# A perceiver block: the first query projection from high and low parts, the rotation's addition on GpSimd, scores laid out by chunk

## The reference

```
q_hk  = (layernorm(x) @ Wq.T)          # 16 heads of 128
q_big = einsum(q_hk, w_kc_q)           # per head: 128 -> 384
q_big = rope(q_big)                    # x*cos + rotate_half(x)*sin
q_r   = einsum(q_big, W_qr)            # per head: 384 -> 64
kv_r  = rope(ctx);  k_r = einsum(kv_r, W_kr)
p     = softmax(q_r @ k_r.T)           # 16 heads, 256 x 4096
out   = (p @ kv_r, then w_kc_kv, then Wo)
```

## Time and profile before

| | us |
|---|---|
| median of the runs | 1048.62 |
| the profiled execution, its time | 1046.65 |
| its span | 1044.70 |
| TensorE busy | 990.0 |
| VectorE busy | 734.7 |
| ScalarE busy | 575.3 |
| GpSimd busy | 290.8 |

### The profile page before, as it was taken

One profiled execution on the slowest core, in us unless ns is written; L12 is line 12 of the kernel. 1 busy time (PEld: TensorE's weight loads), 2 busy tenths in 40 slices (PEclk: granted clock), 3 DMA queues, 4 the chain that ended last, 5 costly groups with the idle time before them and its releaser, 6 DMA issues.

```text
span 1044.7 us, 17977 instructions
## 1 busy us (share of the span) xinstructions
PE 990.0 (95%) x6612; PEld 789.3 (76%) x6612; DVE 734.7 (70%) x1449; ACT 575.3 (55%) x1257; POOL 290.8 (28%) x210
## 2 busy tenths in 40 slices
PE   7999999999999799999999999999999999989996
PEld 5545689999997667588777878878888787868643
DVE  2566546555553679888887987978877787648555
ACT  3435344444442320287767767776676777836633
POOL 6910054444442300000002222422405423013422
PEclk9999999999999899999999999999999999999998
DMA  8560067665531332121013443424313203074100
GB/s 273 128 244 1 3 197 263 220 220 216 211 121 51 98 101 88 43 82 59 21 24 77 81 129 49 102 41 92 84 37 96 72 1 97 1 274 193 66 1 20
DMA packets 65981, 109.16 MB, mean 104 GB/s; under 512 B 19409, under 2 KB 44145, under 8 KB 64754
## 3 DMA queue, kind: packets, MB, share of 16 engines
q1 hardware_dynamic: 65906, 108.17, 34.0%
HBM read 103.24 MB, written 4.91 MB: 104 GB/s over the span
## 4 chain that ended last, share of the span: by engine, by line
PE 77%; DVE 13%; ACT 5%; issue 2%; DMA 1%; POOL 1%; SPq 0%; DVEq 0%; POOLq 0%; ACTq 0%
PE PS L1658 16%; PE PS L1531 12%; PE PS L1647 10%; PE PS L1635 8%; PE PS L1550 6%; PE PS L1620 4%; PE PS L1750 3%; DVE scores L1164 2%; PE PS L1672 2%; ACT scores L840 1%; PE PS L1431 1%; PE PS L1793 1%; PE PS L1590 1%; PE PS L1379 1%; PE PS L1599 1%
## 5 line engine op out<-in xcount | busy, mean ns | idle before, releaser
L1217 DVE TENSOR_TENSOR pL<-PS,pH 128x512 fp32r<-128x512 f32 x256 | 175.8, 687 | 63.3 <-ACT pH L864 62.9
L864 ACT ACTIVATE pH<-PS 128x512 fp32r<-128x512 f32 x256 | 151.8, 596 | 100.2 <-PE PS L1647 100.2
L840 ACT ACTIVATE scores<-scores,nmX 128x512 f32<-128x512 f32 x256 | 185.2, 724 | 18.5 <-DVE nmX L1168 18.5
L1164 DVE TENSOR_SCALAR_CACHE_REDUCE scores<-PS 128x512 f32<-128x512 f32 x256 | 172.5, 682 | 14.6 <-PE PS L1635 14.3
L1658 PE MATMUL PS<-pH,kvH 128*128 128x256 f32 x512 | 164.6, 321 | 6.6 <-ACT xnT L849 6.6
L1647 PE MATMUL PS<-ident,scores 128*128 128x128 f32 x1024 | 157.1, 276 | 1.1 <-DVE pL L1217 0.9
L1658 PE MATMUL PS<-pL,kvH 128*128 128x256 f32 x512 | 144.0, 281 | 0.0
L1658 PE MATMUL PS<-pH,kvL 128*128 128x256 f32 x512 | 143.7, 281 | 0.0
L1647 PEld LDWEIGHTS PS<-ident,scores 128*128 128x128 f32 x1024 | 117.5, 140 | 31.7 <-issue 16.4
L1658 PEld LDWEIGHTS PS<-pH,kvH 128*128 128x128 f32 x512 | 96.9, 189 | 10.8 <-issue 10.6
L1658 PEld LDWEIGHTS PS<-pL,kvH 128*128 128x128 f32 x512 | 97.3, 190 | 0.0
(11 more groups left out here) (307 smaller groups left out, 2256.0 us busy)
## 6 DMA issues: line engine op xcount, KB each, us to landing
rawG<-in_wg SPq DMA_DIRECT2D x16, 768.0 KB, 5.6
rawU<-in_wu SPq DMA_DIRECT2D x16, 768.0 KB, 7.2
rawD<-in_wd SPq DMA_DIRECT2D x16, 768.0 KB, 6.2
wrow<-in_w SPq DMA_DIRECT2D x11, 512.0 KB, 4.4
xn<-in_w1t SPq DMA_DIRECT2D x11, 512.0 KB
wturned<-turned SPq DMA_DIRECT2D x4, 1056.0 KB, 13.4
wb<-w_rows SPq DMA_DIRECT2D x32, 128.0 KB, 3.3
wqX<-in_wqX SPq DMA_DIRECT2D x16, 256.0 KB, 2.5
```

The lines of the kernel that those rows point to most:

```text
L840: act.activation(at, at, ACT.Exp, bias=nmX[:, p % 2, h, q:q + 1], accum_out=csum[:, p % 2, NT * h + q, c:c + 1]).then_inc(exp_done, 1)
L864: act.activation(pH[:, i % 4], PS[:, 2 + i % 2, :].rearrange("p (k t) -> p k t", t=T), ACT.Copy).then_inc(pH_ready, 1)
L1164: dve.tensor_scalar(sp_[:, h, q, c * CH:(c + 1) * CH], PS[:, 4 * q + h, :], 1.0, None, ALU.mult, ALU.max, accum_out=cmax[:, h, q, c:c + 1] ...
L1217: dve.tensor_tensor(pL[:, i % 4], PS[:, 2 + i % 2, :].rearrange("p (k t) -> p k t", t=T), pH[:, i % 4].bitcast(F32), ALU.subtract).then_in ...
```

## The change

There are four parts.

1. `p1` is made from high and low parts. ScalarE makes the high part `xtH` of the transposed input and `wqH` of each head's weights (128x512); VectorE makes `xtL`; GpSimd makes `wqL` (`low_query`). TensorE runs twelve fp32r matmuls in place of four fp32 ones, and `p1(n)` waits for `low_query(n)` (by `d_ready`) where it waited for the weights' DMA.
2. The sum `qb + qm2` moves from VectorE to GpSimd (`rotated(n)` there), and GpSimd's list gets a loop of 16 rounds.
3. The scores of the first pair come one round later (7 to 14), the scores are laid out by chunk, and `xtH` and `wqH` lie in the room of the last chunk, whose copies therefore wait for the last `p1`.
4. The idle matmuls of round 14 go, and the ones after the loop wait for a copy of scores.

```diff
--- before.py
+++ after.py
@@ -42,7 +42,7 @@
 SLOTS = 2 * NCH
 HALVES = 4 * NCH
 KEYS_AT = {2: (0, 1), 3: (2, 3), 4: (4, 5), 5: (6, 7)}
-SCORES_AT = {6 + c: c for c in range(NCH)}
+SCORES_AT = {7 + c: c for c in range(NCH)}
 TILES = ((0, 0), (1, 0), (0, 1), (1, 1))
 TILES_LAST = ((0, 0), (0, 1), (1, 0), (1, 1))
 JOBS1, JOBS = GT // 2, GT // 2 + DT
...
@@ -185,7 +192,15 @@
         qsH, qsL = (A(n, [P, 2, T], F32R) for n in ("qsH", "qsL"))
         wkr = A("wkr", [P, 2, P]); wkrH, wkrL = (A(n, [P, 2, P], F32R) for n in ("wkrH", "wkrL"))
         rounding = A("rounding", [P, 2])
-        sp_ = A("scores", [P, 2, NT, L])
+        score_chunks = A("scores", [P, NCH - 1, 2, NT, CH])
+        early = ExitStack()
+        xtH = sb("xtH", [P, KT, T], F32R, early); wqH = sb("wqH", [P, 2, KT, XK], F32R, early)
+        early.close()
+        last_chunk = A("last_chunk", [P, 2, NT, CH])
+
+        def score(h, q, c):
+            return last_chunk[:, h, q] if c == NCH - 1 else score_chunks[:, c, h, q]
+
         cmax = A("cmax", [P, 2, NT, NCH]); nmX = A("nmX", [P, 2, 2, NT]); csum = A("csum", [P, 2, 2 * NT, NCH]); recX = A("recX", [P, 2, 2 * NT])
         both = arena
         arena = ExitStack()
@@ -599,14 +614,31 @@
             split_down(0, 0, 0)
             pairs(pool, pool_pair)
             rstd(3)
+
+            def low_query(n):
+                pool.wait_ge(wH_ready, 2 * PAIRS + n + 1)
+                pool.tensor_tensor(wqL[:, n % 2], wqX[:, n % 2], wqH[:, n % 2].bitcast(F32), ALU.subtract).then_inc(d_ready, 1)
+
+            low_query(0)
+            low_query(1)
             pool.wait_ge(kvH_ready, 1)
             pool.tensor_tensor(kvL[:], kvr[:], kvH[:].bitcast(F32), ALU.subtract).then_inc(kvL_ready, 1)
 
-            def low_parts(p):
+            def low_ranks(p):
                 pool.wait_ge(wkrH_ready, p + 1)
                 pool.tensor_tensor(wkrL[:, p % 2], wkr[:, p % 2], wkrH[:, p % 2].bitcast(F32), ALU.subtract).then_inc(wkrL_ready, 1)
+
+            def low_turned(p):
                 pool.wait_ge(qsH_ready, p + 1)
                 pool.tensor_tensor(qsL[:, p % 2], qr[:, p], qsH[:, p % 2].bitcast(F32), ALU.subtract).then_inc(qsL_ready, 1)
+
+            def low_parts(p):
+                low_ranks(p)
+                low_turned(p)
+
+            def rotated(n):
+                pool.wait_ge(qm_ready, n + 1)
+                pool.tensor_tensor(qb[:, n % 4], qb[:, n % 4], qm2[:], ALU.add).then_inc(qb_ready, 1)
 
             def round_columns(k):
 
@@ -626,7 +658,13 @@
 
             step(pool.memset(rounding[:], ROUND))
             for p in range(2):
-                low_parts(p)
+                low_ranks(p)
+            for n in range(XH):
+                if n and n + 1 < XH:
+                    low_query(n + 1)
+                rotated(n)
+                if n in (5, 7):
+                    low_turned((n - 5) // 2)
             pool.wait_ge(qr_ready, XP)
             for p in range(XP):
                 if p + 2 < XP:
@@ -790,10 +828,20 @@

             act.wait_ge(x_done, 3)
+
+            def high_query_weights(n):
+                act.wait_ge(wqX_in[n % 2], (n // 2 + 1) * 16)
+                act.activation(wqH[:, n % 2], wqX[:, n % 2], ACT.Copy).then_inc(wH_ready, 1)
+
             for c in range(NCH):
                 if c == 4:
                     for t in range(NT):
                         turned_tile(3, t, 4)
+                        half = slice(t * P, (t + 1) * P)
+                        act.wait_ge(xnT_ready, 3 * NT + t + 1)
+                        act.activation(xtH[:, :, half], xnT[:, :, half], ACT.Copy).then_inc(xH_ready, 1)
+                    high_query_weights(0)
+                    high_query_weights(1)
                 act.wait_ge(kvT_ps, c + 1)
                 act.activation(kvTH[:, c * CH:(c + 1) * CH], PS[:, c % 4, :], ACT.Copy).then_inc(kvTH_ready, 1)
             act.activation(kvH[:], kvr[:], ACT.Copy).then_inc(kvH_ready, 1)
@@ -823,6 +871,8 @@
                 act.wait_ge(p1_done, n + 1)
                 wait(act, p2_done, n - 1)
                 act.activation(qh[:, n % 2], PS[:, 6, 0:T], ACT.Copy).then_inc(qh_ready, 1)
+                if n and n + 1 < XH:
+                    high_query_weights(n + 1)
                 for c in KEYS_AT.get(n - 1, ()):
                     if c == 0:
                         act.wait_ge(kvL_ready, 1)
...
@@ -1136,6 +1186,11 @@
                 dve.wait_ge(kvTH_ready, c + 1)
                 dve.tensor_tensor(kvTL[:, c * CH:(c + 1) * CH], PS[:, c % 4, :], kvTH[:, c * CH:(c + 1) * CH].bitcast(F32),
                                   ALU.subtract).then_inc(kvTL_ready, 1)
+                if c == 4:
+                    for t in range(NT):
+                        dve.wait_ge(xH_ready, NT + t + 1)
+                        half = slice(t * P, (t + 1) * P)
+                        dve.tensor_tensor(xtL[:, :, half], xnT[:, :, half], xtH[:, :, half].bitcast(F32), ALU.subtract).then_inc(xL_ready, 1)
             dve.wait_ge(qtab_in, 32)
 
             def rotated(n):
@@ -1149,8 +1204,6 @@
                 dve.tensor_tensor(qm2[:, 1], big[:, 0], sinQ[:, 1], ALU.mult)
                 dve.tensor_tensor(qm2[0:LEFT, 2], big[LEFT:P, 2], sinQ[LEFT:P, 2], ALU.mult)
                 dve.tensor_tensor(qm2[LEFT:P, 2], big[0:LEFT, 2], sinQ[0:LEFT, 2], ALU.mult).then_inc(qm_ready, 1)
-                dve.wait_ge(qm_ready, n + 1)
-                dve.tensor_tensor(qb[:, n % 4], qb[:, n % 4], qm2[:], ALU.add).then_inc(qb_ready, 1)
 
             def low_keys(p, c, bank=7):
                 dve.wait_ge(keyH_ready, p * NCH + c + 1)
...
@@ -1195,6 +1248,8 @@
                 for c in KEYS_AT.get(n, ()):
                     low_keys(0, c, 0 if c % 2 else 7)
                 if n in SCORES_AT:
+                    if SCORES_AT[n] == NCH - 1:
+                        dve.wait_ge(p1_done, XH)
                     for e in range(4):
                         scores_out(0, SCORES_AT[n], e)
             low_keys(1, 0)
@@ -1581,13 +1636,14 @@
                 turn_context(c)
             pe.wait_ge(xnT_ready, 4 * NT)
 
-            def p1(n, i, b):
-
-                pe.wait_ge(wqX_in[b], (i + 1) * 16)
+            def p1(n, b):
+
+                pe.wait_ge(d_ready, PAIRS + n + 1)
                 wait(pe, qh_ready, n)
                 wait(pe, qr_ready, (n - 3) // 2)
                 for kt in range(KT):
-                    mm = pe.matmul(PS[:, 6, 0:T], wqX[:, b, kt, :], xnT[:, kt, :], start=(kt == 0), stop=(kt == KT - 1))
+                    for c, (w, v) in enumerate(((wqH, xtH), (wqH, xtL), (wqL, xtH))):
+                        mm = pe.matmul(PS[:, 6, 0:T], w[:, b, kt], v[:, kt], start=(kt == 0 and c == 0), stop=(kt == KT - 1 and c == 2))
                 mm.then_inc(p1_done, 1)
 
             def p2(n, i, b):
@@ -1621,7 +1677,8 @@
                 mm.then_inc(key_ps, 1)
 
             pe.wait_ge(kvTL_ready, NCH)
-            p1(0, 0, 0)
+            pe.wait_ge(xL_ready, 2 * NT)
+            p1(0, 0)
             def scores(p, c):
 
                 if c == 0:
...
@@ -1673,8 +1730,8 @@
 
             for n in range(XH):
                 if n + 1 < XH:
-                    p1(n + 1, (n + 1) // 2, (n + 1) % 2)
-                if n >= XH - 2:
+                    p1(n + 1, (n + 1) % 2)
+                if n == XH - 1:
                     stay_awake(10, 7)
                 p2(n, n // 2, n % 2)
                 if n % 2 and n >= 3:
@@ -1686,6 +1743,7 @@
                     pe.wait_ge(keyL_ready, NCH)
                     scores(0, SCORES_AT[n])
             keys(1, 0)
+            pe.wait_ge(sX_out, 4 * (NCH - 1) + 1)
             stay_awake(6, 0)
             p3(XP - 1)
```

More of the change, by code:

```diff
@@ L109, in perceiver @@
         xn = sb("xn", [P, NT, D])
+        early = ExitStack()
+        xtL = sb("xtL", [P, KT, T], F32R, early)
+        early.close()
         xnT = sb("xnT", [P, KT, T])
@@ L131, in perceiver @@
         keys_room = sb("keys_room", [P, 2 * L], F32, early)
+        wqL = sb("wqL", [P, 2, KT, XK], F32R, early)
+        early.close()
+        early = ExitStack()
+        sb("keys_room2", [P, 2 * L], F32, early)
         wqX = sb("wqX", [P, 2, KT, XK], F32, early)
@@ L838, in exps @@
                     act.wait_ge(nm_ready, 4 * p + 2 * h + q + 1)
-                at = sp_[:, h, q, c * CH:(c + 1) * CH]
+                at = score(h, q, c)
                 act.activation(at, at, ACT.Exp, bias=nmX[:, p % 2, h, q:q + 1], accum_out=csum[:, p % 2, NT * h + q, c:c + 1]).then_inc(exp_done, 1)
@@ L1163, in scores_out @@
                 dve.wait_ge(sX_ps, 2 * (p * NCH + c) + q + 1)
-                dve.tensor_scalar(sp_[:, h, q, c * CH:(c + 1) * CH], PS[:, 4 * q + h, :], 1.0, None, ALU.mult, ALU.max,
+                dve.tensor_scalar(score(h, q, c), PS[:, 4 * q + h, :], 1.0, None, ALU.mult, ALU.max,
                                   accum_out=cmax[:, h, q, c:c + 1]).then_inc(sX_out, 1)
@@ L1645, in turn @@
                     for m in range(2):
```

(4 more changed lines are left out.)

## The result

| | before | after |
|---|---|---|
| median of the runs, us | 1048.69 (4 runs) | 1121.17 (4 runs, 1118.09 to 1122.94) |
| the profiled execution | 1046.65 | 1120.1 |
| its span | 1044.7 | 1118.4 |
| p2(1) to p2(14), first product to first product | 77.1 | 136.5 |
| TensorE busy | 990.0 | 1012.1 |

The ratio of the runs is 1.0704, with a 95% interval of 1.0674 to 1.0733. The changed kernel is slower; the forecast was 1114 in a range of 1090 to 1128.

What follows compares the result with a forecast made beforehand. VectorE was taken to bound the score rounds. 13 rounds of 10.15 us plus two subtractions, starting 10.8 later, put p2(14) +65.5 later; with +1.8 at the end, 1046.65 became 1114 us, range 1090 to 1128.

Steps and rivals of the forecast that it cites:

- The series: From p2(n-1) to p2(n): products, GpSimd's addition and low part, then p1 run one after another; 8.75 us a round against 6.05.
- the ring: The same loop of waits: p1 behind GpSimd's low part, that behind the addition, that behind VectorE's products, these behind p2.
- The lead of ScalarE: ScalarE's high parts, four copies ahead of the first round, then one of 0.6 us a round, were to cost nothing.
- Ahead of the rounds: Up to p2(1): kvH starts 1.0 us later, kvL delays GpSimd's first addition, p1(2) runs at half clock; +10.8 us.
- The clock: TensorE's idle gap in each round brings a half-clock stretch covering about p1 alone; 1.4 us a round, making 10.15.
- The end: From p2(14) to the last p3: 11.1 us where it was 9.3, so +1.8.
- Full clock (1094): Rival: the clock stays at 2.4 GHz, rounds of 8.75 us, 1094 us; chance 0.20.
- The addition hidden (1044): Rival: GpSimd's low part is done ahead of its addition, score rounds of 5.1 instead of 5.84 us, 1044; chance 0.07.
- The port: VectorE's xtL subtraction meets GpSimd's first two low parts and loses up to 2 x 1.28 us; the sum stays.

Runs made afterwards that it cites:

- e5: The changed kernel with idle matmuls on TensorE in each round's gap ahead of p1; 1097.88 us, ratio 1.0477 to the kernel before.
- e1: The changed kernel with GpSimd's low part for head n+2 put ahead of the addition of round n; 1051.07 us, ratio 1.0046 to the kernel before.
- e11: The changed kernel with p2(n) put ahead of p1(n+1) on TensorE, GpSimd's order kept; 1058.27 us, ratio 1.0097 to the kernel before.
- e10: As e8, but VectorE makes xtL ahead of the products of round 6; 1041.65 us, ratio 0.9950 to the kernel before.
- e8: As e6, but p1 from parts only from head 8 on, with xtL made in round 6; 1049.45 us, ratio 1.0019 to the kernel before.
- e6: The changed kernel with low part ahead of addition, p1 from parts only from head 4, GpSimd adding only from round 6; 1048.22 us, ratio 1.0014.

## Why the prediction was right, step by step

- *The series.* Right in every piece, to 0.1 us. Forecast and measured at full clock in e5: p1 until p2 starts 1.44 and 1.52, p2 until the first product 1.5 and 1.49, first product to addition 2.52 and 2.57, addition 1.84 and 1.80, low part 1.28 and 1.26, the round 8.75 and 8.66. The trace shows the ring, e1 and e11 cut it at either of its two orders, and the loss goes. Shown. Only the sign given for it was too narrow: p1 was to wait 3 to 4 us in each round, and waited 2.65 to 5.75.
- *The lead of ScalarE.* Right inside the rounds: GpSimd's low parts waited for ScalarE only ahead of round 0. There its new copies were put at nothing, and that was wrong; see *Ahead of the rounds*.
- *The clock.* Right as a mechanism, its size too small: 1.4 us a round taken, 1.72 measured (10.50 - 8.78). The term stood for p1 alone at half clock. The chain has p1 at 2.20 to 2.93 (1.68 at full clock) and p2 at 1.53 to 2.57 (1.31), and in the last five rounds p2 pays more than p1. The reason given for p1 alone, that the slow stretch begins inside the idle time, doesn't hold in these rounds, where the clock is full until p1 has begun. Over 13 rounds the term is 4.2 us short; the series with the low parts of two rounds was 1.1 too long, which leaves the 3.1 of the table. The Trainium skill (TensorE: Matmul & The Clock Gate, section "HAM oscillation — how this bites in real kernels") says that a loop whose bursts are shorter than its waits restarts slowly in every turn. The slow turns came here: from the start of p1 to the first product the 14 rounds took 4.4 to 5.5 us, and 3.0 in e5. But TensorE's bursts were the longer part, 79.94 us of 125, so the condition that was taken from that page wasn't met.
- *Ahead of the rounds.* +10.8 forecast, +12.2 measured, and 0.9 of this is that the stage began later. The path was another than forecast, and that the sum came near is luck. The addition was to wait for kvL, and p1(0) was to be done before ScalarE was through with kvH. The trace has it otherwise:

```profile
345.07 3.64 ACT L847 ACTIVATE kvH<-kvr 128x4096 fp32r<-128x4096 f32 x1
...
347.65 0.55 PE L1646 MATMUL PS<-xtH,wqH 128*128 128x256 f32 x1 [4.81 <-DVE kvTL L1187]
...
356.68 0.96 DVE L1202 TENSOR_TENSOR qb<-PS,cosQ 128x768 f32<-128x768 f32 x1 [9.13 <-PE PS L1655]
```

p1(0) starts at 347.65, before at 343.31. It waits for VectorE's low parts of the context rows (kvTL). Those wait for ScalarE's copies, which stand behind its new ones, one of which waited 1.2 us for the weights' DMA, and VectorE's new subtractions (1.37) stand ahead of the last three. kvH starts 2.7 us later and not 1.0. After its idle time TensorE ran p1(0), p1(1) and p2(0) at half clock (0.50 from 347.6 to 356.6), so the products of round 0 came at 356.68, before at 350.18, and the addition waited for them until 359.25. GpSimd had been free since 358.65: kvL, which began at 348.79 and not 347.1, would have held it nearly as long, with the two small subtractions at 0.87 and not 1.5. Two paths ended within 0.6 us of each other, and the forecast had one of them.
- *The end.* +1.8 forecast, +3.4 measured: p2(14) too ran at half clock, some 1.1 us longer, and from p2(15) to its first product it was 2.1 us and not 1.5.
- *The rivals.* Full clock (1094) is what e5 made: 1097.88. The addition hidden (1044) had a condition, the low part ahead of the addition, that e1 sets up: 1051.07. Its rounds came nearly as priced (5.3 for 5.1), but it counted 3.4 us for the late start, where 8.7 were measured. e10 with 1041.65 isn't this rival: it also leaves heads 0 to 7 and the first six additions as before.
- *The port.* The rule of the Trainium skill (SBUF — State Buffer, section "Who interferes with whom") was weighed at a place where it decided nothing. e8 has a better one: VectorE's two subtractions with two SBUF inputs and GpSimd's addition start together at 386.11 and 386.16 and take 2.90 and 2.30. The addition takes 1.80 by itself, and the two subtractions took 1.29 in e10 (at 380.42, where GpSimd started nothing for their first us). That agrees with turns of whole instructions: 0.5 of waiting for GpSimd, the second subtraction behind it.

## What to carry to other kernels

Engines that work through lists in order make a ring when an instruction on one waits for the tail of a list on another whose head waits for work behind that instruction: follow each new wait once around before adding it, and put work that depends on little (a low part, a copy of weights) ahead of work that depends on much. Such a ring shows in the profile as every engine waiting for the next about once a round while none is full, and it cost twice here, since the gap also took TensorE's clock. I made the same mistake twice more in e6 and e8, in a smaller form, and only the row of the wait showed it.

## What the runs showed of the hardware that was not expected

The granted clock falls at different places of the round. In rounds 3 to 5 and 10 to 14, as in the round shown, it is full through the idle time and falls after p1 has begun. In rounds 1, 2 and 6 to 9 it falls in the idle time, and p1 runs at half clock from its first matmul (0.58 us for 0.39). Round 2, ahead of p1 at 373.13:

```profile
371.00:373.00 2.00, 0.00 (x0) 0.00 (x0) 0.00 (x0) 0.00 (x0) 2.00 (x2) 0.50 0.00 0
```

The length of the idle time doesn't tell the two kinds apart: it is 2.65 to 4.31 us ahead of the first and 3.33 to 5.75 ahead of the second. And of the 14 intervals between GpSimd's additions up to 506.57 eight take 10.24 to 10.30 us, three in rounds 2 to 5 and the last five; the others take 10.12 to 11.87. In the last five p1 grows from 2.20 to 2.38 and p2 shrinks from 2.42 to 2.22, with a sum of 4.60 to 4.62. How the clock and the round fall into step was not tried.
